# Groups of 3, 3, 4, 3, 3 weight tiles in place of 2, 3, 4, 4, 3, and delta units in the startup's halves

## The reference, cut to what matters

```
lora_delta = lora_B @ lora_A * 0.5
normalized = (weight + lora_delta) / scale                 # 2048 x 2048, groups of 128
quantized = cb[searchsorted(thresholds, normalized)]       # 31 thresholds
w_eff = quantized * scale + lora_delta
h = x @ w_eff.T
result = h @ W_base.T + b_base                             # plus, from ax = h @ A_w.T and
                                                           # softmax(h @ router_w.T), the experts'
out = x + result                                           # rank-16 part
```

## Time and profile before

| what | value |
| --- | --- |
| median of three runs | 2499.61 us (2494.25 to 2500.36) |
| the profiled execution | 2502.43 us, its span 2500.6 us |
| PE busy | 2373.2 us, 95% |
| DVE busy | 1795.6 us, 72% |
| ACT busy | 1499.5 us, 60% |
| POOL busy | 1203.9 us, 48% |
| mean granted TensorE clock | 0.987 |

### The profile page before, as it was taken

The page is one execution under the profiler, slowest core; times in us unless marked ns, Lnnn a source line. Parts: engine busy times, 40 slices in busy tenths (PEclk is TensorE's granted clock), DMA queues, the critical chain, the costliest instruction groups (busy, mean ns, idle before and its releaser), DMA issues.

```text
span 2500.6 us, 31530 instructions
## 1 busy us (share of the span) xinstructions
PE 2373.2 (95%) x11808; PEld 2129.7 (85%) x11808; DVE 1795.6 (72%) x2274; ACT 1499.5 (60%) x1906; POOL 1203.9 (48%) x742
## 2 busy tenths in 40 slices
PE   5688998899999999999999999999999999999999
PEld 2345777787988899999999999899999989899998
DVE  5898998698899987858878858866666634344444
ACT  5898999677788857657666636654544414311111
POOL 3677877544688763436776633444554310010010
PEclk9999999999999999999999999999999999999999
DMA  4565556544788773345666643446665544456665
GB/s 157 184 231 182 206 201 214 183 141 143 250 288 294 286 257 115 114 135 211 238 227 231 226 169 103 119 143 218 223 238 212 211 142 131 140 215 234 237 239 199
DMA packets 141981, 493.06 MB, mean 197 GB/s; under 512 B 15058, under 2 KB 75986, under 8 KB 100818
## 3 DMA queue, kind: packets, MB, share of 16 engines
q1 hardware_dynamic: 141828, 491.05, 56.8%
HBM read 305.91 MB, written 185.07 MB: 196 GB/s over the span
## 4 chain that ended last, share of the span: by engine, by line
PE 77%; DVE 11%; ACT 5%; issue 2%; POOL 2%; DMA 2%; SPq 0%; DVEq 0%; POOLq 0%; ACTq 0%
PE m L621 17%; PE m L622 17%; PE m L623 17%; DVE acc L879 9%; PE m L605 8%; PE m L606 8%; PE m L607 8%; PE pd L559 2%; ACT mk L739 2%; PE m L651 1%; DMA part<-part 1%; ACT mp L749 1%; POOL pp L1024 1%; ACT ds L727 1%; DVE kl L906 1%
## 5 line engine op out<-in xcount | busy, mean ns | idle before, releaser
L879 DVE SCALAR_TENSOR_TENSOR acc<-mk,dj,acc 128x1024 f32<-128x1024 uint8 x800 | 1025.1, 1281 | 117.8 <-ACT mk L739 53.6
L739 ACT ACTIVATE mk<-wr,bj 128x1024 uint8<-128x1024 f32 x800 | 902.6, 1143 | 232.7 <-DVE acc L879 222.5
L621 PE MATMUL m<-gh,xh 128*128 128x384 f32 (+2 forms) x2560 | 913.7, 357 | 25.6 <-DVE part L896 11.3
L622 PE MATMUL m<-gl,xh 128*128 128x384 f32 (+2 forms) x2560 | 902.6, 353 | 0.0
L623 PE MATMUL m<-gh,xl 128*128 128x384 f32 (+2 forms) x2560 | 900.3, 352 | 0.0
L621 PEld LDWEIGHTS m<-gh,xh 128*128 128x128 f32 x2560 | 484.2, 189 | 84.2 <-issue 24.7
L623 PEld LDWEIGHTS m<-gh,xl 128*128 128x128 f32 x2560 | 483.7, 189 | 23.4
L622 PEld LDWEIGHTS m<-gl,xh 128*128 128x128 f32 x2560 | 484.8, 189 | 20.6
L1020 POOL TENSOR_SCALAR tm<-mp,dj 128x1024 f32<-128x1024 uint8 x192 | 218.3, 1137 | 452.6 <-ACT mp L749 448.3
L901 DVE TENSOR_TENSOR part<-m,part 128x384 f32<-128x384 f32 (+2 forms) x480 | 280.2, 585 | 215.3 <-PE m L623 214.8
L605 PE MATMUL m<-kh,wh 128*128 128x384 f32 (+2 forms) x1120 | 398.6, 356 | 25.6 <-DVE kl L906 17.4
(11 more groups left out here) (88 smaller groups left out, 1439.1 us busy)
## 6 DMA issues: line engine op xcount, KB each, us to landing
part<-part SPq DMA_DIRECT2D x256, 1036.0 KB, 4.8
kw<-in_wb SPq DMA_DIRECT2D x192, 192.0 KB, 2.4
rows<-in_wb SPq DMA_DIRECT2D x32, 1036.0 KB, 4.8
out<-part SPq DMA_DIRECT2D x32, 1024.0 KB, 4.0
wr<-in_w SPq DMA_DIRECT2D x32, 512.0 KB, 5.9
kw<-in_wb SPq DMA_DIRECT2D x64, 256.0 KB, 2.6
xw<-in_x SPq DMA_DIRECT2D x64, 256.0 KB, 3.1
dl<-delta SPq DMA_DIRECT2D x30, 512.0 KB, 5.8
```

The costliest lines, as they stand in the source:

```text
L621: e.matmul(R.m[c][:, 0:w], xh, gh, start=k == 0, stop=False)
L622: e.matmul(R.m[c][:, 0:w], xh, gl, start=False, stop=False)
L739: e.activation(R.mk[k % NM], w, ACT.Identity, bias=R.bj[:, j:j + 1], scale=GROW).then_inc(S["mk"], 1)
L879: e.scalar_tensor_tensor(R.acc, R.mk[k % NM], R.dj[:, j:j + 1], R.acc, ALU.mult, ALU.add).then_inc(S["ac"], 1)
```

## The change

`GROUP` becomes (3, 3, 4, 3, 3). G0 has three tiles, G3 three. The startup holds halves 0 to 6. The token stage of G0 holds halves 7 to 11, the stages of G1 12, 13 and 14 to 19, those of G2 20, 21 and 22 to 25, those of G3 26, 27 and 28 to 31. Of the 48 later delta units twelve stand in halves 1 to 6, at units 3 and 5, and 36 in halves 7 to 15: 20 in the token stage of G0, 8 in the weight stage of G1 and 8 in its token stage (before 20, 8 and 20).

```diff
--- before.py
+++ after.py
@@ -31,7 +31,7 @@
 GROW = float(2.0 ** 100)
 FULL = 255.0
 
-GROUP = (2, 3, 4, 4, 3)
+GROUP = (3, 3, 4, 3, 3)
 NG = len(GROUP)
 FIRST = tuple(sum(GROUP[:g]) for g in range(NG + 1))
 GC_BEFORE = tuple(NCH * sum(n - 1 for n in GROUP[1:max(g, 1)]) for g in range(NG))
@@ -277,7 +277,7 @@
 
     places = {(0, 1): ("direct", 2), (0, 3): ("direct", 3)}
     places.update({(0, 5 + n): ("delta", n) for n in range(16)})
-    late = [(q, j) for q in range(2 * N0 + 1, NQ) for j in (3, 9, 15, 21)]
+    late = [(q, j) for q in range(1, NQ) for j in ((3, 5) if q <= 2 * N0 else (3, 9, 15, 21))]
     places.update({at: ("delta", 16 + n) for n, at in zip(range(NDELTA - 16), late)})
     return places
```

## The result

The changed kernel takes 2536.02 us, the median of four runs, against 2499.02: a ratio of 1.0151, interval 1.0132 to 1.017. The profiled execution took 2539.2 us (span 2537.4). The forecast was 2500 us in a range of 2482 to 2518.

What follows compares the result with a forecast made beforehand. PE was taken to bound the kernel from G1 on, quantisation on DVE and ACT before that. The terms 76.7 + 3 + 56.4 - 2.4 - 8.1 - 36.3 - 89.0 gave +0.3 us: 2500 us, range 2482 to 2518.

Steps and rivals of the forecast that it cites:

- The startup grows by 76.65 us: Startup: seven halves instead of five are quantised before G0's tokens; halves 5 and 6 add 76.65 us.
- Twelve units for 3 us (0 to 33): Startup: twelve delta units moved into halves 1 to 6 cost +3 us; 0 if all hidden, 33 at 2.75 each.
- The rival that they are exposed: Startup: PE and ACT take turns on the moved delta units, delaying masks; 2530 us, half of it 2513; chance 0.13.
- G0's tokens 298 us, PE the limit, clock 1.00: Token stage of G0, two tiles to three: PE replaces DVE and ACT as limit; 298 us, +56.4, bounds 295 and 310.
- The 4.1 us that I had added for a slow begin and for the remainder: G0's tokens: 1.7 us for a slow first matmul, 2.4 us left over from the same working for G1's tokens.
- G1's weights -2.4: Weight stage of G1 with the gap before it: 163.2 to 160.8 us, -2.4, within 4 either way.
- G1's tokens 285: Token stage of G1, 8 deltas instead of 20: 285 us, -8, part kept as DVE time; bounds 281 and 293.
- G3's weights 150: Weight stage of G3, one tile fewer: 186.3 to 150 us, -36.3, above 144 because of DVE; 154 at the most.
- the rule: G3's weights: VectorE's two-input subtractions contend with POOL's SBUF reads; 8.8 us more for DVE, 154 instead of 150 if DVE limits.
- G3's tokens -89.0: Token stage of G3, four tiles to three: 361.5 us becomes 271.1 and 1.4 for a wait, -89.0; halves fill DVE only partly.
- G2 and G4 unchanged: Stages of G2 and G4 keep their size: 0, unchanged to a microsecond.
- The third, DVE and POOL: Short stages bound by DVE and POOL: G1's tokens 293, G3's weights 154, G0's tokens 302; 2516 us; chance 0.12.

Runs made afterwards that it cites:

- the kernel with the common wait: Against the kernel with the partial result in two pieces at the old places, SP's first-piece load also waits until both stored pieces have landed; 2527.8 us, 1.0111.

## Why the prediction was wrong, step by step

- *The startup grows by 76.65 us:* right, 76.9 with the deltas.
- *Twelve units for 3 us (0 to 33):* right in kind, near the lower end at 0.2. The rival that they are exposed did not come in the change, but the mechanism is real: it costs 46 us where a unit stands behind the rows. I counted ACT's free time per half and had the right argument only by the place ahead of the rows; the expectation for the kernel with units at 9, 15 and 21 shows that I didn't carry it through.
- *G0's tokens 298 us, PE the limit, clock 1.00:* right, 294.6 and 1.00. The 4.1 us that I had added for a slow begin and for the remainder were nearly all too much: the first matmul took 0.41 us, not 0.66.
- *G1's weights -2.4:* -3.5. The sum came out better than its parts: the gap fell from 5.5 to 2.5 us and not to 0.8, and PE's longest wait for a slice was 3.8 us and not 5.4.
- *G1's tokens 285:* 293.5 in this execution. In five kernels that share everything up to here the stage took 286.4 to 297.9 us, one execution each. In the two that took 286.4 and 286.5 it is near the 285 of the forecast, with every half without deltas at 44.5 to 44.6 us, as DVE's own pace said, and SP waited 4.6 and 4.8 us a token for a landing. In the three of 293 and more it waited 6.1 to 6.5 us, and in two of them, the changed kernel and the one without POOL's spare work in G3's weights, the last two halves took 46 to 50 us. So SP's loop goes with the loss here as well; what sends one execution into it and not another stays open. The kernel with the common wait (292.6 us, against 286.3 and 288.0 with a wait for each piece) lies inside this spread and doesn't settle it.
- *G3's weights 150:* 156.8, over the bound of 154. The term was DVE's load and POOL's reach into it; I had worked the rule out to 154 and thought the milder case likelier.
- *G3's tokens -89.0:* this step failed. I scaled the stage by its tiles, 3/4 of 361.5, and looked only at whether DVE had room (221 of 361 us). SP's queue and the transfers don't scale with tiles: the load and store of 2 MB a token stay. In the trace of the kernel before, SP waited 4.7 us a token for a landing and had 5.4 of slack; a token 2.8 us shorter uses up half of that, and the longer wait for the landing, 3.2 us more, the rest. The rates were a hint as well: 213 GB/s at four tiles makes some 276 at PE's pace for three, with the smaller loads of x taken off. The rate itself is not the limit, since G1's tokens ran at 282 GB/s before and those of G3 at 273 in pieces. G1's tokens had 9.2 us a token thanks to the delta units, with only 1.7 us of SP's slack left; I read their length as PE's alone.
- *G2 and G4 unchanged:* right, to 2 us.

The errors sum up: -3 in the startup, -3 in G0's tokens, -1 in G1's weights, +8, +7, +24 and +7 in the three places, -2 in G2 make +37, the whole miss. None of my rivals had this mechanism. The third, DVE and POOL, came nearest in its numbers for G1's tokens (293) and G3's weights, but not for G3's tokens.

## What to carry to other kernels

When a stage loses matmuls, list what doesn't shrink with them, each transfer and each wait of the issuing queue, and work out its rate at the new pace; an engine's free time says nothing about that. A queue that waits for a store's landing before it issues the reload is a serial loop through the transfer engines: cut the tile in pieces, so that one is in flight while the other is waited for. And a small step moved into another phase is free only ahead of the long work in every queue that it passes.

## What the runs showed of the hardware

The 1036 KB transfers of G3's token stage landed in 4.8 us (median of loads and stores) at 11.3 us a token and in 6.3 at 9.3 us a token; the stores alone went from 5.0 to 8.3 us, and SP's wait for one from 4.7 to 7.9. The same bytes moved at 248 GB/s with whole tiles, 252 with pieces behind one common wait, and 273 with each piece behind its own. VectorE's subtraction of a 384-column slice took 557 ns (mean) with POOL nearly idle, 662 with POOL's spare work cut, and 922 beside all of it.
